# Mixture on rows sorted by expert: the first feed-forward stage of a graph transformer, blocks of 128 rows with weights addressed by a register

## The reference, cut to what matters

```python
gate_logits = xf @ Wg + bg                       # (8*1024, 8)
top_w, top_i = jax.lax.top_k(gate_logits, 2)
top_w = jax.nn.softmax(top_w, axis=-1)
w_dense = jnp.sum(one_hot(top_i, E) * top_w[..., None], axis=1)
for e in range(E):                               # E = 8
    h = gelu(xf @ W1[e] + b1[e], approximate=False)      # 128 -> 512
    out = out + w_dense[:, e:e+1] * (h @ W2[e] + b2[e])  # 512 -> 128
```

## Time and profile before

| | |
|---|---|
| median of three runs | 3047.97 us |
| the profiled execution | 3052.26 us |
| its span, first to last instruction | 3050.2 us |
| granted TensorE clock, mean | 0.932 |
| TensorE (PE) busy | 2532.1 us, 83% |
| VectorE (DVE) busy | 1840.7 us, 60% |
| ScalarE (ACT) busy | 1340.0 us, 44% |
| GpSimd (POOL) busy | 865.5 us, 28% |

### The profile page before, as it was taken

The page is one execution under the profiler, slowest core; times in us unless marked ns, Lnnn a source line. Parts: engine busy times, 40 slices in busy tenths (PEclk is TensorE's granted clock), DMA queues, the critical chain, the costliest instruction groups (busy, mean ns, idle before and its releaser), DMA issues.

```text
span 3050.2 us, 48344 instructions
## 1 busy us (share of the span) xinstructions
PE 2532.1 (83%) x16137; PEld 1511.7 (50%) x16137; DVE 1840.7 (60%) x5404; ACT 1340.0 (44%) x1993; POOL 865.5 (28%) x917
## 2 busy tenths in 40 slices
PE   0039559888799989998899889998899999997796
PEld 0026436444466445654466445654566556644253
DVE  5345467874686558764686557865686188318603
ACT  1024224166434653366435653366425553552163
POOL 4737536307500472017400572007500000000000
PEclk9989869889899999999999999999999999998697
DMA  6626666327401372118411483117411120021000
GB/s 148 81 45 82 79 110 82 52 67 107 72 29 44 78 117 37 43 56 111 65 42 41 83 105 41 43 56 128 49 42 36 25 46 28 29 42 36 22 1 7
DMA packets 107565, 183.69 MB, mean 60 GB/s; under 512 B 21471, under 2 KB 57724, under 8 KB 107260
## 3 DMA queue, kind: packets, MB, share of 16 engines
q0 software_dynamic: 25344, 51.96, 19.0%
q1 hardware_dynamic: 81916, 128.08, 15.3%
HBM read 158.59 MB, written 20.97 MB: 59 GB/s over the span
## 4 chain that ended last, share of the span: by engine, by line
PE 37%; DVE 34%; issue 13%; DVEq 6%; ACT 4%; DMA 3%; SPq 2%; ACTq 0%
DVE tmp L1124 14%; PE PY L1396 7%; PE PH L1386 7%; PE PA L1431 5%; PE PA L1434 5%; PE PY L1445 4%; DVE G L902 2%; DMA adj_sb<-in_adj 2%; DVE res_f L1026 2%; PE PA L1408 2%; DVEq L822 2%; ACT HB L1258 2%; DVE res_n L1026 2%; SPq L748 2%; DVE score L870 2%
## 5 line engine op out<-in xcount | busy, mean ns | idle before, releaser
L794 POOL DMA_INDIRECT G<-table,slot_idx x792 | 839.0, 1059 | 262.6 <-issue 258.7
L1124 DVE CUSTOM_DVE_ANT_0 tmp<-PA,mask 128x1024 bf16<-128x1024 f32 x512 | 626.9, 1225 | 34.8 <-issue 34.8
L1258 ACT ACTIVATE HB<-PA 128x1024 f32<-128x1024 f32 x512 | 498.1, 1022 | 328.2 <-PE PA L1434 327.0
L1251 ACT ACTIVATE HB<-PH,bias_T 128x512 f32<-128x512 f32 x512 | 351.4, 687 | 613.3 <-PE PH L1386 613.1
L1386 PE MATMUL PH<-XT,W_sb 128*128 128x512 f32 x1024 | 521.1, 625 | 33.4 <-ACT HB L1251 16.6
L1396 PEld LDWEIGHTS PY<-W_sb,HB 128*128 128x128 f32 x4096 | 504.5, 192 | 68.9 <-issue 38.5
L1396 PE MATMUL PY<-W_sb,HB 128*128 128x128 f32 x4096 | 509.4, 276 | 2.5 <-DVE res_n L1026 2.5
L1431 PE MATMUL PA<-QS,KS 99*128 99x512 bf16 x1024 | 407.1, 398 | 12.0 <-ACT HB L1258 7.6
L1434 PE MATMUL PA<-identb,mask 128*128 128x128 bf16 x4096 | 410.6, 224 | 0.0
L1434 PEld LDWEIGHTS PA<-identb,mask 128*128 128x128 bf16 x4096 | 328.2, 100 | 135.9 <-issue 19.2
L1408 PE MATMUL PA<-KS,QS 96*128 96x512 bf16 x1024 | 335.1, 412 | 54.2 <-DVE MX L1124 46.8
(11 more groups left out here) (163 smaller groups left out, 2388.3 us busy)
## 6 DMA issues: line engine op xcount, KB each, us to landing
adj_sb<-in_adj SPq DMA_DIRECT2D x64, 512.0 KB
adjm<-in_adj SPq DMA_DIRECT2D x64, 512.0 KB
G<-table,slot_idx POOLq DMA_INDIRECT x792
parts_dram<-parts SPq DMA_DIRECT2D x16, 768.0 KB, 3.5
QS<-parts_dram SPq DMA_DIRECT2D x96, 128.0 KB, 5.6
KS<-parts_dram SPq DMA_DIRECT2D x96, 128.0 KB, 7.9
xn<-in_x SPq DMA_DIRECT2D x8, 512.0 KB, 5.3
table<-xn SPq DMA_DIRECT2D x8, 512.0 KB, 4.3
```

The costliest lines, as they stand in the source:

```text
L794: pool.indirect_dma_start(G[:, t % 2, s, :], None, table, bass.IndirectOffsetOnAxis(slot_idx[:, t, s:s + 1], axis=0), bounds_check=ROWS - ...
L1124: ins = dve.tensor_tensor_reduce(out=junk, in0=psum(ps, step)[:, :], in1=mask[:, t, :], scale=1.0, scalar=LOWEST, op0=ALU.add, op1=ALU.max ...
L1251: act.activation(HB[:, i % 2, c, :], psum(ps, step)[:, :], ACT.Gelu, bias=bias_T[:, e * HC + c:e * HC + c + 1]).then_inc(*emptied(ps, step))
L1258: act.activation(HB[:, kc % 2, 2 * pr:2 * pr + 2, :], psum(ps, key)[:, :].rearrange("p (h q) -> p h q", h=2), ACT.Exp, scale=float(D) ** - ...
```

## The change

The first mixture is computed only for the two experts that a row chose. `rank` (TensorE, nine small products with a strictly triangular and an all-ones matrix on the marks `chosen`) counts, for every row, how many rows before it chose the same expert. `dest` (VectorE, `places`) turns this into a row number in an order sorted by expert, in which each expert's rows begin at a multiple of 128; 2048 rows and eight experts fill at most BLOCKS = 16 + 7 = 23 blocks of 128 rows, in QUADS = 6 groups of four. It also writes the expert of each block (`block_at`) and one bias column per block and hidden quarter (`bias_of`). `scatter` (GpSimd, 16 indirect DMAs of 128 rows) writes the normed rows to a DRAM buffer in this order. Per group, `xs` loads the rows, `xT` transposes them. Per block, `up` reads the block's expert into a register of TensorE and multiplies the rows with the 512 columns of `W1_sb` at the address in the register; ScalarE copies the product out; `ut` transposes its four quarters; ScalarE applies Gelu to each with its own bias; `dn` multiplies with `W2_sb` at the register's address. Per group, `ye` copies the result and `ys` stores it. `collect` (GpSimd, 16 indirect DMAs) fetches each row's two results and `mix` (VectorE, 16 scaled additions) adds them to `res_n`. `up0`, `down0` and `acc0` go.

The input of a graph is loaded, normed and stored to the table one pass earlier (part `ahead`, graph g+4, with one more pass at the start, g = -4, so that the loop has four turns instead of five); it lies in the memory of `XT`, and `again` reads the normed rows back from the table. The DRAM buffer of sorted rows is zeroed once at the start. Of the score maxima those of heads 0 to 3 on the first four tiles come first and may start after `fina` of the second attention group; heads 4 to 7 of these tiles follow after tile 3. `mT` uses one place instead of two. The planner gets durations and ranks for the new steps. In the diff each part is shown without its common indentation.

```diff
-ORDER0 = [(hf, e) for hf in range(2) for e in range(E0)]
 ORDER1 = [(hf, e) for hf in range(2) for e in range(E1)]
-N0, N1 = len(ORDER0), len(ORDER1)
+N1 = len(ORDER1)
+BLOCKS = 2 * NODES // P + E0 - 1
+QUADS = (BLOCKS + HTILES - 1) // HTILES
+SORTED = QUADS * HALF
...
-EXPERTS = ("up0", "down0", "u1", "u2", "y1")
-LEAD = {"u1": 10.0, "u2": 10.0, "y1": 10.0}
+EXPERTS = ("xT", "up", "ut", "dn", "u1", "u2", "y1")
+ON_POOL = ("gather", "scatter", "collect")
+LEAD = {"xT": 20.0, "up": 20.0, "ut": 20.0, "dn": 20.0}
 LANDING = 3.0
-EAGER = {"acc0": 3.0, "acc1": 3.0, "find": 2.0, "pmax": 2.0, "s": 1.2}
+EAGER = {"scatter": 3.0, "collect": 3.0, "acc1": 3.0, "find": 2.0, "pmax": 2.0, "s": 1.2}
...
+        if load:
+            p.gate(("qT",), ("class", 0))
+if ahead:
+    p.chain([("load_x",), ("lnv", 0), ("sq", 0), ("ln", 0), ("store_x",)])
+    p.gate(("load_x",), ("up", BLOCKS - 1) if near else None)
+    p.gate(("lnv", 0), ("ln", 3) if att else None, ("ln", 1) if near else None)
+    p.gate(("store_x",), ("pmax", TILES - 1) if load else None, ("again",) if load else None)
...
-    line += [("s", t, h) for h in range(HEADS)]
+    line += [("s", t, h) for h in range(GH if t < HTILES else HEADS)]
+    if t == HTILES - 1:
+        line += [("s", early, h) for early in range(HTILES) for h in range(GH, HEADS)]
 if att:
-    p.gate(("mask", 0), ("finc", 1, 1))
-    p.gate(("mask", TILES - 2), ("u1", N1 - 1))
+    p.gate(("mask", 0), ("fina", 0, 1))
+    p.gate(("mask", HTILES), ("finc", 1, 1))
...
+p.threads.append([("scatter",), ("collect", 0), ("collect", 1)])
+p.gate(("scatter",), ("dest",))
+p.gate(("collect", 0), ("pmax", TILES - 2) if load else None)
+for q in range(QUADS):
+    p.gate(("xs", q), ("scatter",), ("xT", q - 2) if q >= 2 else last_av)
+    p.gate(("xT", q), ("xs", q), ("lg0",), ("up", HTILES * (q - 1) - 1) if q >= 2 else None)
+    p.gate(("ye", q), ("dn", min(HTILES * (q + 1), BLOCKS) - 1), ("ys", q - 2) if q >= 2 else None)
+    p.gate(("ys", q), ("ye", q))
+    p.gate(("collect", 0), ("ys", q))
+p.threads.append([("xs", q) for q in range(QUADS)])
+p.threads.append([("ye", q) for q in range(QUADS)])
+p.threads.append([("ys", q) for q in range(QUADS)])
+blocks = [("xT", 0)]
+for j in range(BLOCKS + 2):
+    if j < BLOCKS:
+        if j % HTILES == HTILES - 2 and j // HTILES + 1 < QUADS:
+            blocks.append(("xT", j // HTILES + 1))
+        blocks.append(("up", j))
+        p.gate(("up", j), ("xT", j // HTILES))
+    if 1 <= j <= BLOCKS:
+        blocks.append(("ut", j - 1))
+        p.gate(("ut", j - 1), ("up", j - 1))
+    if j >= 2:
+        blocks.append(("dn", j - 2))
+        p.gate(("dn", j - 2), ("ut", j - 2))
+p.threads.append(blocks)
+p.threads.append([("mix", 0), ("mix", 1)])
+for h in range(2):
+    p.gate(("mix", h), ("collect", h), ("ba", 0))
+if att:
+    p.gate(("ln", 3), ("scatter",))
+if unit:
+    p.gate(("mparts",), ("dn", BLOCKS - 1))
...
+hid = [flat[:, i * HALF:(i + 1) * HALF] for i in range(2)]
+xrows = [flat[:, (2 + i) * HALF:(3 + i) * HALF].rearrange("p (r c) -> p r c", c=C) for i in range(2)]
+raw = [flat[:, (6 + i) * HALF:(7 + i) * HALF] for i in range(2)]
+yrows = [flat[:, (4 + i) * HALF:(5 + i) * HALF] for i in range(2)]
+YG = G[:, 0, 0:2 * TILES, :].rearrange("p (i t) c -> p i t c", i=2)
+XR = XT[:, :].rearrange("p (t c) -> p t c", c=C)
+bias_of = mparts[:, :, :].rearrange("p k n -> p (k n)").bitcast(F32).rearrange("p (k n) -> p k n", k=PARTS)
+XF = XB
...
+for q in range(QUADS):
+    sp.dma_start(xs_dram[q * HALF:(q + 1) * HALF, :].rearrange("(r p) c -> p r c", p=P),
+                 bias_diag[:, :, :]).then_inc(s_zero, 16)
+sp.wait_ge(s_zero, 16 * QUADS)
...
 if kind == "load_x":
     if ps.near:
-        sp.wait_ge(*is_taken(ps, turn, ("xn", 1)))
-    sp.dma_start(xn0[:, :, :], x_v[b + 3, :, :, :]).then_inc(S["xin"], 16)
+        sp.wait_ge(*is_taken(ps, turn, ("up", BLOCKS - 1)))
+    sp.dma_start(XR, x_v[b + 4, :, :, :]).then_inc(S["xin"], 16)
+elif kind == "again":
+    stored = settled(sp, at(ps, turn, "tab"))
+    if ps.near:
+        seen = settled(sp, is_taken(ps, turn, ("xn", 1)))
+        sp.wait_ge(*seen)
+    sp.wait_ge(*stored)
+    sp.dma_start(xn0[:, :, :], table[0:NODES, :].rearrange("(t p) c -> p t c", p=P)).then_inc(S["xrow"], 16)
+elif kind == "xs":
+    q = step[1]
+    if q == 0:
+        sp.wait_ge(*at(ps, turn, "sca", ("scatter",)))
+    if q >= 2:
+        sp.wait_ge(*is_taken(ps, turn, ("xT", q - 2)))
+    elif ps.att:
+        sp.wait_ge(*is_taken(ps, turn, ("av", 1, 1)))
+    sp.dma_start(xrows[q % 2], xs_dram[q * HALF:(q + 1) * HALF, :].rearrange(
+        "(r p) c -> p r c", p=P)).then_inc(S[f"xl{q % 2}"], 16)
+elif kind == "ys":
+    q = step[1]
+    sp.wait_ge(*is_taken(ps, turn, ("yb", q)))
+    sp.dma_start(ys_dram[q * HALF:(q + 1) * HALF, :].rearrange("(r p) c -> p r c", p=P),
+                 yrows[q % 2].rearrange("p (r c) -> p r c", c=C)).then_inc(S[f"yst{q % 2}"], 16)
...
+def scatter(ps, turn):
+    pool.wait_ge(*at(ps, turn, "bk", ("dest",)))
+    pool_held_by(pool, 2 * TILES)
+    for t in range(TILES):
+        for i in range(2):
+            pool.indirect_dma_start(
+                xs_dram, bass.IndirectOffsetOnAxis(dest[:, i, t:t + 1], axis=0), xn[:, t, :], None,
+                bounds_check=SORTED - 1, oob_is_err=False).then_inc(S["sca"], 16)
+def collect(ps, turn, h):
+    if h == 0:
+        if ps.load:
+            pool.wait_ge(*at(ps, turn, "aggr", ("pmax", TILES - 2)))
+            pool_held_by(pool, 2 * TILES + 1)
+        for i in range(2):
+            pool.wait_ge(*at(ps, turn, f"yst{i}", ("ys", QUADS - 2 + i)))
+            pool_held_by(pool, 2 * TILES + 2 + i)
+    for t in range(HTILES):
+        for i in range(2):
+            at_t = h * HTILES + t
+            pool.indirect_dma_start(
+                YG[:, i, at_t, :], None, ys_dram,
+                bass.IndirectOffsetOnAxis(dest[:, i, at_t:at_t + 1], axis=0),
+                bounds_check=SORTED - 1, oob_is_err=False).then_inc(S[f"col{h}"], 16)
...
+def places(ps, turn):
+    dve.wait_ge(*is_full(ps, turn, ("rank",)))
+    ranks = psum(ps, ("rank",))[:, 0:(TILES + 1) * EP].rearrange("p (t e) -> p t e", e=EP)
+    need, a, b = (c[:, :] for c in counts)
+    grid = tmp[:, 0:EP * EP].rearrange("p (e k) -> p e k", k=EP)
+    settle(dve.scalar_tensor_tensor(out=grid, in0=ranks[:, TILES, :].unsqueeze(2).to_broadcast([P, EP, EP]),
+                                    scalar=1.0 / P, in1=eidx[:, :, :], op0=ALU.mult, op1=ALU.is_gt))
+    settle(dve.tensor_reduce(out=need, in_=grid, axis=AX.X, op=ALU.add))
...
+    dve.tensor_copy(dst[:, 0:d], src[:, 0:d])
+    settle(dve.tensor_tensor(dst[:, d:EP], src[:, d:EP], src[:, 0:EP - d], ALU.add))
+    src, dst = dst, (b if dst is a else a)
+upto = src
+settle(dve.tensor_tensor(need, upto, need, ALU.subtract))
...
+block_e = tmp[:, 2 * B * EP:2 * B * EP + B]
+own = tmp[:, 0:B * EP].rearrange("p (j e) -> p j e", e=EP)
+some = tmp[:, B * EP:2 * B * EP].rearrange("p (j e) -> p j e", e=EP)
+settle(dve.tensor_tensor(own, upto.unsqueeze(1).to_broadcast([P, B, EP]),
+                         block_no[:, :].unsqueeze(2).to_broadcast([P, B, EP]), ALU.is_le))
+settle(dve.tensor_reduce(out=block_e, in_=own, axis=AX.X, op=ALU.add))
+settle(dve.tensor_scalar(block_e, block_e, float(E0 - 1), None, ALU.min))
+dve.tensor_copy(block_at[:, :], block_e[0:1, :])
+settle(dve.tensor_tensor(own, block_e.unsqueeze(2).to_broadcast([P, B, EP]),
+                         eidx[:, 0:1, :].to_broadcast([P, B, EP]), ALU.is_equal))
+biases = bias_T[:, 0:E0 * HC].rearrange("p (e c) -> p c e", c=HC)
+cols = bias_of[:, :, 0:B * HC // PARTS].rearrange("p k (j c) -> p c k j", c=HC)
+for c in range(HC):
+    settle(dve.tensor_tensor(some, own, biases[:, c:c + 1, :].to_broadcast([P, B, EP]), ALU.mult))
+    ins = dve.tensor_reduce(out=cols[:, c, :, :], in_=some.rearrange("p (k j) e -> p k j e", k=PARTS),
+                            axis=AX.X, op=ALU.add)
+    if c == HC - 1:
+        ins.then_inc(S["bk"], 1)
+    dve.drain()
...
+def mix(ps, turn, h):
+    dve.wait_ge(*at(ps, turn, f"col{h}", ("mix", h)))
+    for i, w in enumerate((w1st[0], w2nd[0])):
+        for t in range(h * HTILES, (h + 1) * HTILES):
+            dve.scalar_tensor_tensor(out=res_n[:, t, :], in0=YG[:, i, t, :], scalar=w[:, t:t + 1],
+                                     in1=res_n[:, t, :], op0=ALU.mult, op1=ALU.add)
+        dve.drain()
...
 elif kind == "gT":
+    act.wait_ge(*at(ps, turn, "tab"))
...
+elif kind == "xT":
+    q = step[1]
     act.wait_ge(*is_full(ps, turn, step))
-    act.activation(HB[:, i % 2, c, :], psum(ps, step)[:, :], ACT.Gelu,
-                           bias=bias_T[:, e * HC + c:e * HC + c + 1]).then_inc(*emptied(ps, step))
+    act.activation(XT[:, half[q % 2]], psum(ps, step)[:, :],
+                   ACT.Copy).then_inc(*emptied(ps, step))
+elif kind == "up":
+    copy_out(raw[step[1] % 2], ps, turn, step)
+elif kind == "ut":
+    j = step[1]
```

(71 more changed lines are left out.)

291 lines of the change are left out of this document (174 added, 117 removed), and 4 rows, old and new, of the table COURSE.

## The result

The changed kernel takes 3021.26 us (median of four runs, 3011.8 to 3024.31); the kernel before took 3049.95 beside it. The ratio is 0.9904, interval 0.9876 to 0.9932: some 29 us faster, where 259 were forecast. Its profiled execution took 3021.74 us with a span of 3019.7, 30.5 less than before.

The account below looks back on a forecast made before the run. TensorE and VectorE hold each other in turns, TensorE slightly ahead. From a span of 3050.2 us, -221 (full passes), -36, -11 and +9 gave 2791, so 2789 us beside 3047.97; 8-in-10 range 2680 to 2950.

Parts of the forecast that it names:

- The step that failed: Full pass: 340.2 less TensorE's freed 56.7, plus 14.5 for registers, plus 6, minus 8: 296; five times -44.2 = -221.
- Rival 1: Full pass: early maxima find no room and VectorE takes over; pass 306 us, sum 2840 us; chance 0.17.
- The products: First mixture on TensorE: 115.0 us per graph becomes 58.3, so TensorE gives back 56.7 us.
- The register: Expert read and register addresses on TensorE: 0.3 + 0.33 us per block, 14.5 us per pass, ends 0 and 103.
- ScalarE: Gelus and copies: 17 us more on 169 of 340 per pass, hidden; a Gelu of 128 columns 0.436 us.
- VectorE: Net -4.5 us; its last part's work 135 us, 124 with early maxima, 140 at the density where only maxima are left.
- The gap of the sorted rows: Between attention and blocks: rows queue on SP among the stack's loads, so blocks start about 6 us after the attention.
- Early maxima: About eight fit under the attention's end; 8 us off a full pass (0 to 14), -11 with attention and maxima only.
- GpSimd: 32 indirect DMAs, 41.6 us more per pass on 106 busy, hidden in a full pass; fetches behind `scatter` wait 20.8.
- rival 3: Pass end: the chain through DRAM after the last `dn`, 21 us, paid by each of eight passes; 2957 us; chance 0.09.
- Pass 5: The pass without load, 303 us with TensorE at 296: -56.7 + 14.5 + 6 = -36 us.
- rival 4: TensorE's clock granted at 0.8: 138 us would be 172, some +25 us in six passes, 2939 us; chance 0.06.

Follow-up runs that it names:

- before, less of `down0`: Kernel before with three of the four products of each `down0` left out (192 per graph, TensorE), timing only: 2992.29 us, ratio 0.9834.
- before, less of `down0` and `acc0`: Kernel before with three of four products of `down0` and three of four additions of `acc0` left out, timing only: 2930.97 us, ratio 0.9633.
- changed, maxima late: Changed kernel without its reordering: all 64 score maxima after the last attention group again: 3052.80 us, ratio 1.0043.
- early with load: Changed kernel with early score maxima only in passes that load a graph, the old order in the others: 2990.55 us, ratio 0.9836.
- the same, few GpSimd DMAs: Kernel "early with load" with only 2 of 16 scatter DMAs and one of eight in each collect half, timing only: 2922.29 us, ratio 0.9598.

## Why the prediction was wrong

**The step that failed** is the one from engine sums to a pass. The sum takes TensorE's freed time one to one off the full pass (340.2 - 56.7 + 14.5), and the reason given is "the part can't fall below 140, from 200 now". It took the 200 us behind the attention as one basin in which TensorE's 138 and VectorE's 124 could lie beside each other freely, with VectorE at the density of the thin stretch of the earlier trace rows, 0.89. The same cuts in every kernel, means of the five full passes (us; attention from `shift` to the end of the last `av`, then to the end of the last maximum, then to the next `shift`):

| kernel | attention | to the last maximum | rest | pass |
|---|---|---|---|---|
| before | 126.5 | 192.2 | 22.3 | 341.0 |
| before, less of `down0` | 127.2 | 192.4 | 14.7 | 334.3 |
| before, less of `down0` and `acc0` | 126.8 | 183.1 | 13.4 | 323.2 |
| changed, maxima late | 139.1 | 194.6 | 4.8 | 338.5 |
| changed | 152.7 | 164.2 | 9.1 | 326.1 |
| early with load | 150.2 | 165.6 | 9.1 | 324.9 |
| the same, few GpSimd DMAs | 143.2 | 165.5 | 9.0 | 317.7 |

The runs show three pieces behind the attention. (a) A gap of 21 to 27 us in which the stacks are loaded and hardly a maximum can run (none in that of the kernel before). (b) A stretch of 64 maxima with searches and the reduction of neighbours, VectorE at 0.84 before and 0.79 with the maxima late, which set 163 us beside a TensorE that was nearly full too. (c) 24 us of TensorE alone. Up to the last maximum it is 192 us whether TensorE has its work or not; only (c) answers to TensorE. What I called 200 us is 214.5 by these cuts and came to 199 with the maxima late, 173 in the changed kernel, not 140. That stood in the rows: I had read TensorE at 121 of 123 as "TensorE is the bound", and VectorE's 97 beside it as slack. Less work for TensorE in the kernel before, with nothing else changed, gave 4 to 8 us per full pass for 30 to 38, against one to one in the sum. Rival 1 named the mechanism but priced the pass at 306 with the gap left out; it was 326, and 338.5 under rival 1's own condition that no maxima come early.

**The attention** is a second term that the sum put at nothing. With the maxima late it is 13 us longer per full pass, nearly as much as (c) gave back (17.5). In the kernel with early maxima only with load, 7 us of the attention go when scatter and collect are nearly gone.

**The products**: 56.7 us per graph is about what the mixture itself gave back, by luck. Both of its sides were priced in a stretch that was granted the full clock (1.00). Over the whole run the old products were busy 521.1 and 509.4 us, 128.8 per graph instead of 115.0; the new lines (products, transposes, `rank`) are busy 571, that is 71.3 per graph instead of 58.3. The difference is 57.5. TensorE's total fell by less, 49 us per graph (51 in a full pass), because its other work was busy for longer, as I read it by the lower clock: 5.7 of the missing 8.5 us lie in the products of attention and maxima (the score product of the attention took 409 ns instead of 398, that of the maxima 424 instead of 412).

**The register**: 14.5 us per pass were too many, about 1.8 measured.

**ScalarE**: hidden, as forecast, and cheaper. Its busy time rose by 11.5 us in all, not by 17 per pass; a Gelu of 128 columns was busy 210.2/736 = 0.286, less than my 0.436.

**VectorE**: the sum was near (1792.6 from 1840.7, that is 6 less per graph where I had 4.5), the density wrong.

**The gap of the sorted rows**: 6 us taken. TensorE waited 14.6 in the full pass with the maxima late, as the loads stand behind twelve stack loads on SyncE, and the rest was hidden only where early maxima filled it. I named those stack loads and priced one load of 5.3 us, not the queue.

**Early maxima**: taken within 8 us per pass as a plain gain, with eight under the attention; six got there. They gave 62 in the full passes, 12 each, and cost 31 in passes 5 and 6, which I had at nothing and -11: that step passed over what else uses ring A.

**GpSimd**: "hidden in a full pass" was wrong by about 7 us each; in pass -2 scatter was priced (20.8), collect and `mix` were not, although they must follow the last fetch. That is rival 3, true in one pass and not in eight: 42 against 11. **Start-up** was right. **Pass 5** was missed in the changed kernel (-7, forecast -36) by the early maxima; with them late it is -32. There is no search or reduction on VectorE in it, TensorE had 296 of 303 us, and there the freed time does come back. That it comes so near -36 is partly luck, since a register term that is too large stands against an attention 6.5 us longer, which the sum did not have.

**The clock** (rival 4): the granted clock fell from 0.932 to 0.869 over the span, to 0.71 in the gap of the full pass shown. Rival 4's sign, under 0.9 between the last `av` and the next pass, came with the maxima late (0.83 from 1145 to 1348, against 0.97 in the kernel before) and in part in the changed kernel (0.86 to 0.94). I read it as a result of the waits more than a cause of the miss, since less work for TensorE after the change gave nothing; the clock by itself was not tested, and its share of the miss stays open. By the rule of the Trainium skill ("TensorE: Matmul & The Clock Gate", section "HAM oscillation — how this bites in real kernels") the next burst after a wait starts cold; the trace agrees, with the 1.06 us against 0.60 behind the wait of 14.56. By that the wait for rows costs more than its length.

**Still open**: the rest of the longer attention. It is 126.5 us before, 139 with the maxima late and 153 with them early; some 14 come with the early maxima and 7 with the DMAs of scatter and collect, but whether those act by GpSimd's order, the adjacency loads or shared DMA engines no run tells, nor what makes up the last 6. The one attempt on the adjacency load made the order worse.

## What to carry to other kernels

Before crediting an engine's freed time, cut the pass at its own events and ask for every piece which engine would still need that long; the time that a second engine, busy at 0.84, leaves beside a full one is not slack. The cheapest test is to leave that work out of the old kernel: it tells what the time is worth before the replacement is written. And price a new load by what stands ahead of it on its queue, and put the load that one engine waits for ahead of those that nobody needs yet.

## What the runs showed of the hardware

- A block's expert read into a register and used in operand addresses cost about 0.08 us per block (15 us in 184 blocks, and 1.7 us in 22 steps of pass -2), hardly more than the measurement can tell. On TensorE it shows mainly as idle time ahead of weight loads (70.2 against 49.2 us), hardly ahead of products (23.4 against 16.7).
- A Gelu of 128 columns took 0.286 us of ScalarE's busy time in rows of four, where the two larger sizes of the earlier trace rows had led me to 0.436.
- Work taken from both engines gave 20 us, from one 7 or nothing. That two engines which feed each other through small rings have to be relieved together is suggested by this, not shown: the intervals of the one and the other touch, and most of the time taken off came back in neither case.
- In this kernel the same two bf16 products of 512 columns took 1.06 us in a stretch granted 0.62 of the clock, behind a wait of 14.56 us, and 0.60 us once the clock was granted in full.
